# Window attention on one core: out products of a block's windows in one matmul, with the own window selected afterwards

## What is computed

```
qkv = jnp.einsum('nchw,oc->nohw', xw, qkv_w)
pooled = _avg_pool5(qkv)
msq = jnp.concatenate([qkv, pooled], axis=1)
msq = msq.reshape(N, -1, 3 * DIM, ws * ws).transpose(0, 1, 3, 2)
q = jax.nn.relu(msq[..., :DIM])
k = jax.nn.relu(msq[..., DIM:2 * DIM])
v = msq[..., 2 * DIM:]
v = jnp.pad(v, ((0, 0), (0, 0), (0, 0), (0, 1)), constant_values=1.0)
kv = jnp.einsum('ngld,nglm->ngdm', k, v)
out = jnp.einsum('ngld,ngdm->nglm', q, kv)
out = out[..., :-1] / (out[..., -1:] + 1e-15)
...
y = jnp.einsum('nchw,oc->nohw', out, proj_w)
inv = bn_gamma / jnp.sqrt(bn_var + BN_EPS)
y = y * inv[None, :, None, None] + (bn_beta - bn_mean * inv)[None, :, None, None]
```

## Time and profile before

| | |
|---|---|
| median of 3 runs | 887.09 us (884.8 to 888.21) |
| the profiled execution | 886.18 us |
| its span in the trace | 884.3 us |
| granted TensorE clock, mean | 0.998 |
| TensorE busy, matmuls | 848.4 us (96%) |
| VectorE busy | 699.9 us (79%) |
| GpSimd busy | 658.9 us (75%) |
| ScalarE busy | 480.9 us (54%) |
| TensorE matmul instructions | 28322 |

### The profile page before, as it was taken

One profiled execution on the slowest core, in us unless ns is written; L12 is line 12 of the kernel. 1 busy time (PEld: TensorE's weight loads), 2 busy tenths in 40 slices (PEclk: granted clock), 3 DMA queues, 4 the chain that ended last, 5 costly groups with the idle time before them and its releaser, 6 DMA issues.

```text
span 884.3 us, 63772 instructions
## 1 busy us (share of the span) xinstructions
PE 848.4 (96%) x28322; PEld 693.0 (78%) x28322; DVE 699.9 (79%) x1252; ACT 480.9 (54%) x1349; POOL 658.9 (75%) x1624
## 2 busy tenths in 40 slices
PE   0789999999999999999999999999999999999997
PEld 0568888888888888888888888888888888888885
DVE  7758888887778888888777888888777777777776
ACT  0346565646465655555555556565656564646563
POOL 2558787878787878777878777787878787878781
PEclk9999999999999999999999999999999999999999
DMA  6122322111123323111113232211111111111111
GB/s 236 40 77 81 103 84 82 49 47 48 47 69 97 91 94 98 51 48 47 49 50 99 86 98 88 82 51 48 48 50 46 49 48 47 48 47 48 47 49 47
DMA packets 39081, 60.06 MB, mean 68 GB/s; under 512 B 8560, under 2 KB 33648, under 8 KB 39024
## 3 DMA queue, kind: packets, MB, share of 16 engines
q1 hardware_dynamic: 39024, 59.52, 20.0%
HBM read 19.38 MB, written 18.87 MB: 43 GB/s over the span
## 4 chain that ended last, share of the span: by engine, by line
PE 94%; DVE 3%; issue 1%; DMA 1%; SPq 0%; ACT 0%; DVEq 0%
PE ps L703 24%; PE ps L687 17%; PE ps L659 14%; PE ps L668 9%; PE ps L675 9%; PE ps L787 7%; PE ps L778 6%; PE ps L789 4%; PE ps L676 4%; DVE stats L453 1%; DMA x_all<-x 0%; DVE kvc_full L561 0%; DVE kvc_pool L561 0%; DMA vm_full<-v_full 0%; DVE kvc_full L509 0%
## 5 line engine op out<-in xcount | busy, mean ns | idle before, releaser
L366 ACT ACTIVATE vm_pool<-ps,cst 128x256 f32<-128x256 f32 x576 | 230.1, 480 | 0.0
L376 ACT ACTIVATE q_full<-ps 128x384 f32<-128x384 f32 x96 | 47.2, 491 | 281.0 <-PE ps L675 281.0
L561 DVE TENSOR_TENSOR kvc_full<-ps,cst 128x864 f32<-128x864 f32 x192 | 193.2, 1048 | 4.7 <-PE ps L687 4.7
L561 DVE TENSOR_TENSOR kvc_pool<-ps,cst 128x864 f32<-128x864 f32 x192 | 193.2, 1048 | 0.5 <-PE ps L687 0.5
L286 POOL TENSOR_TENSOR xd<-x_all,mean_t 128x384 f32<-128x384 f32 x95 | 78.6, 827 | 154.3 <-PE ps L676 137.8
L659 PE MATMUL ps<-wkv_sb,xn 128*128 128x256 f32 x576 | 141.4, 382 | 23.1 <-DVE xn L517 23.1
L264 POOL TENSOR_TENSOR x_all<-y_pool,x_all 128x96 f32<-128x96 f32 x380 | 148.9, 424 | 12.7 <-DVE x_all L567 7.2
L659 PEld LDWEIGHTS ps<-wkv_sb,xn 128*128 128x128 f32 x576 | 109.4, 191 | 33.2 <-issue 23.0
L703 PEld LDWEIGHTS ps<-kvc_full,q_full 64*32 64x32 f32 x9216 | 108.3, 105 | 26.0 <-issue 26.0
L292 POOL TENSOR_TENSOR xn<-xd,rstd_t 128x96 f32<-128x96 f32 x380 | 121.8, 367 | 8.1 <-DVE xn L517 0.7
L703 PE MATMUL ps<-kvc_full,q_full 64*32 64x72 f32 x9216 | 125.0, 230 | 0.6 <-DVE kvc_pool L561 0.6
(11 more groups left out here) (74 smaller groups left out, 1316.2 us busy)
## 6 DMA issues: line engine op xcount, KB each, us to landing
vm_full<-v_full SPq DMA_DIRECT2D x384, 54.0 KB, 1.9
out<-x_all SPq DMA_DIRECT2D x96, 192.0 KB, 1.9
x_all<-x SPq DMA_DIRECT2D x36, 384.0 KB, 3.4
x_all<-x SPq DMA_DIRECT2D x6, 768.0 KB, 7.9
cst<-consts SPq DMA_DIRECT2D x1, 170.0 KB, 11.0
wkv_sb<-wkv SPq DMA_DIRECT2D x1, 128.0 KB, 10.8
o_sb<-proj SPq DMA_DIRECT2D x1, 128.0 KB, 10.1
wq_sb<-wq SPq DMA_DIRECT2D x1, 64.0 KB, 10.6
```

The costliest lines, as they stand in the source:

```text
L366: last = act.activation(heads[:, e, :, :, 0:D], src, ACT.Copy, scale=col(C_VP + e))
L561: last = dve.tensor_tensor(kvc[:, g], src.to_broadcast(shape), own, ALU.mult)
```

## The change

It changes how the out products of a quad's windows are told apart, who prepares their right-hand sides, and in which order and banks the steps run.

- An out product takes all windows of the quad at once: `out_tile` multiplies a quad's q (no zeros beside it) with the kv matrices of both windows, 144 columns in one matmul instead of two accumulated ones of 72. Each output row then holds a block for its own window and one for the other.
- The pooled ones (`pooled_out_tile`) contract over one quad's 32 partitions instead of 64, with the three windows' 108 columns, in two halves j = 0 and 1. So `kvc_pool` needs no copies with zeros for the other quad: `own_heads_pooled` is now four ScalarE instructions, one for each head column block, with a per-partition scale that is 1 for the channels of that head and 0 for others. It leaves VectorE.
- VectorE picks each row's own window: `select` copies window 0 and then, where a row belongs to window 1, copies window 1 over it (`copy_predicated`); `select_pooled` does so for three windows. Both write to `sel` in SBUF.
- One `divide` for full and pooled together reads `sel` and writes `o`.
- PSUM banks are free when the selection is over: `kv_products_pooled` waits for `sel_f`, `conv_kv` for `sel_p`. Banks: `TRF` and `Y_F` move to 7, `TRP` to 4, `Y_P` to 0.
- TensorE's order: pooled half 0, full, pooled half 1, then kv products. The transposes wait for `num`, `qm_f` and `qm_p`; the pooled projection waits for the first half of the next `kvc_full`; the full kv products wait for `copy_y_pooled`.
- VectorE's order: residual, select, select pooled, divide, `own_heads` of the next strip, statistics. ScalarE's: `own_heads_pooled` first, and `pooled_out` after `relu_k`.

The diff, cut to its core:

```diff
 def own_heads_pooled(s):
+    act.wait_ge(kv_p, s + 1)
+    wait(act, out_p, s)
+    src = ps[:, KVP:KVP + G, 0:HALF * KC].rearrange("p g (w c) -> p g w c", c=KC)
+    for h in range(4):
+        cols = slice(h * HC, (h + 1) * HC)
+        last = act.activation(kvc_pool[:, :, :, cols], src[:, :, :, cols], ACT.Copy,
+                              scale=col(C_HEAD + h))
+    last.then_inc(kvc_p, 1)
...
+def select(s):
+    dve.wait_ge(out_f, s + 1)
+    wait(dve, num, s)
+    dve.tensor_copy(sel_f_part, full_windows(0)).then_inc(win_f, 1)
+    dve.wait_ge(win_f, s + 1)
+    dve.copy_predicated(sel_f_part, rows_of(1, [P, G, TF, QG * KC]), full_windows(1)).then_inc(sel_f, 1)
+
+def select_pooled(s):
+    dve.wait_ge(out_p, s + 1)
+    dve.tensor_copy(sel_p_part, pooled_windows(0)).then_inc(win_p, 1)
+    dve.wait_ge(win_p, s + 1)
+    for e in range(1, WP):
+        dve.copy_predicated(sel_p_part, rows_of(WF + e, [P, G, TP * QG, KC]),
+                            pooled_windows(e)).then_inc(sel_p, 1)
+        dve.wait_ge(sel_p, (WP - 1) * s + e)
...
 def step(s, b, at, phase):
-    own_heads(s, False)
-    own_heads(s, True)
+    if not is_first(s):
+        residual(s - 1)
+    select(s)
+    select_pooled(s)
+    divide(s)
+    if not is_last(s):
+        own_heads(s + 1)
...
-    if not is_first(s):
-        residual(s - 1)
-    if not is_last(s):
-        divide(s, False)
-    divide(s, True)
...
+def out_tile(t):
+    n = WF * QG * KC
     for g in range(G):
         rows = slice(H64 * g, H64 * (g + 1))
         for c in range(4):
+            r, w = c // QG, (t * QG + c % QG) * WF
+            last = pe.matmul(ps[Q4 * c:Q4 * (c + 1), OUTF + g, t * n:(t + 1) * n],
+                             q_full[rows, 4 * t + c], kvc_full[rows, r, w:w + WF],
+                             start=True, stop=True)
...
+def pooled_out_tile(t, j):
+    n = WP * KC
+    for g in range(G):
+        rows, at = slice(H64 * g + Q4 * j, H64 * g + Q4 * (j + 1)), (t * QG + j) * n
...
 def kv_products_pooled(s):
     pe.wait_ge(vm_p, s + 1)
-    wait(pe, num_f, s)
+    wait(pe, sel_f, s)
...
 def transposes(s):
+    pe.wait_ge(num, s + 1)
     if not is_last(s):
-        pe.wait_ge(kvc_f, s + 2)
+        pe.wait_ge(qm_f, s + 2)
...
 def step(s, p):
...
     conv_kv_pooled(s + 1, p)
     if not is_first(s):
-        project(s - 1, out_next=True)
+        project(s - 1)
+    out_pooled(s, 0)
     out_products(s)
-    out_products_pooled(s)
+    out_pooled(s, 1)
     kv_products(s + 1)
     kv_products_pooled(s + 1)
     conv_q(s + 1, p)
```

More of the change, by code:

```diff
@@ L549, in link, with own_heads @@
                 dve.wait_ge(dv, s * DV + n)
[L551 to L556, removed]
+            def own_heads(s):
+                dve.wait_ge(kv_f, s + 1)
+                wait(dve, out_f, s)
                 shape = [P, HALF, QG, KC]
@@ L559, in own_heads @@
                 for g in range(G):
[L560 to L562 removed]
+                    src = ps[:, KVF + g, 0:HALF * KC].rearrange("p (w c) -> p w c", c=KC).unsqueeze(2)
+                    dve.tensor_tensor(kvc_full[:, g], src.to_broadcast(shape), own, ALU.mult).then_inc(kvc_f, 1)
             def residual(s):
@@ L584, in residual_pooled_last, with rows_of @@
                 last.then_inc(y_done, 1)
[L586 to L590, removed]
-                src = ps[:, bank:bank + G, 0:tiles * QG * KC].rearrange("p g (n c) -> p g n c", c=HC)
-                link(dve.tensor_scalar(den[:], src[:, :, :, D], DEN_EPS, None, ALU.add), s, step + 1)
-                link(dve.reciprocal(den[:], den[:]), s, step + 2)
-                wait(dve, turned, s)
-                heads = [P, G, tiles * QG * 4, D]
+            def rows_of(window, shape):
+                return col(C_WIN + window).bitcast(mybir.dt.uint32).unsqueeze(2).unsqueeze(3).to_broadcast(shape)
@@ L754, in out_products_pooled, with out_products, transposes @@
+            def out_products(s):
+                pe.wait_ge(kvc_f, G * (s + 1))
+                pe.nop(nofuse=True)
+                for t in range(TF):
+                    last = out_tile(t)
+                last.then_inc(out_f, 1)
+            def transposes(s):
+                pe.wait_ge(num, s + 1)
+                if not is_last(s):
+                    pe.wait_ge(qm_f, s + 2)
                 else:
                     pe.wait_ge(added_f, s)
-                    pe.wait_ge(y_copied, s)
@@ L758, in out_products_pooled @@
-                    pe.nop(nofuse=True)
-                for t in range(TP):
-                    for e in range(WP):
-                        last = out_tile(True, t, e)
-                last.then_inc(out_p, 1)
-            def transposes(s):
-                if not is_last(s):
-                    pe.wait_ge(kvc_f, s + 2)
-                else:
-                    pe.wait_ge(num_f, s + 1)
-                    pe.wait_ge(added_f, s)
-                    pe.wait_ge(y_copied, s)
-                for bank, o, n, pxs, columns, done in (
-                        (TRF, o_full, TF, P, C_IDENT, tr_f), (TRP, o_pool, TP, 4 * WP * PXP, C_PACK, tr_p)):
-                    if is_last(s) and o is o_pool:
-                        pe.wait_ge(num_p, s + 1)
-                    for t in range(n):
-                        last = pe.transpose(ps[:, bank, t * pxs:t * pxs + P], o[:, t].rearrange("p c g -> p (c g)"),
-                                            col(columns, P))
-                    last.then_inc(done, 1)
@@ L782, in project @@
-            def project(s, out_next=False):
+                for t in range(TF):
+                    last = pe.transpose(ps[:, TRF, t * P:(t + 1) * P], o[:, t].rearrange("p c g -> p (c g)"),
+                                        col(C_IDENT, P))
+                last.then_inc(tr_f, 1)
+                if not is_last(s):
+                    pe.wait_ge(qm_p, s + 2)
+                pxs = 4 * WP * PXP
+                for t in range(TP):
+                    last = pe.transpose(ps[:, TRP, t * pxs:t * pxs + P], o[:, TF + t].rearrange("p c g -> p (c g)"),
+                                        col(C_PACK, P))
```

136 lines of the change are left out of this document (74 added, 62 removed).

## The result

The changed kernel takes 938.42 us (median of 4 runs, 936.64 to 941.65) against 887.64 us of the kernel before beside it: a ratio of 1.058, 95% interval 1.0545 to 1.0621. It is slower by 5.8%. The forecast was 875 us with a range of 858 to 906, so the time lies outside it, and it moved the other way: slower instead of faster.

A forecast was written before the change was run, and what follows sets the result against it. TensorE was taken to bound the kernel, busy 96% of the span, 8.77 us a strip. From 886.2 us, 94 strips x 0.11 and 0.5 for start and tail were subtracted: 875 us, range 858 to 906.

The forecast's parts named there:

- the second loop, through the division: VectorE's copies, joint division and product up to TensorE's transposes: margin 0.08 us, 8.58 us as a loop of its own.
- the product of 640 elements at 0.83 us: VectorE's last division step, sized from 559 ns for 384 elements and 1.04 ns an element; ends at 5.49.
- GpSimd and the DMA queue keep their work: Work of GpSimd and the DMA queue taken as unchanged; spreading of values takes up to 2.4 us, in time.
- TensorE, what is removed: Out products per strip: 2.20 us replaced by 0.73 full and 0.74 pooled; TensorE's own work falls from 8.77 to 8.04 us.
- Changes of the shape: TensorE switching between whole-array, 32x32 and 64x32 tiles: three changes more a strip, 0.15 us each, bounds 0 and 0.18.
- Where VectorE's answer becomes late: TensorE's pooled kv products wait for VectorE's selection: a new wait of 0.17 us, next beat at 8.66 us.
- The predicated copies: VectorE's selection copies, taken at 1.04 ns an element: 0.60 us for 432 elements, 0.45 for 288.
- the bound taken from the residual: Dearer estimate for the predicated copy of 432 elements, from the residual's 0.62 us for 384: 0.67 us; 0.60 was taken.
- Rival 3: Predicated copies are dear and VectorE sets the beat: slower from 1.23 ns an element, 911 to 967 us; chance 0.26.
- Its sign for failure in the profile: In the trace after the change, TensorE's transposes wait for VectorE's product `o`; no size given.
- ScalarE: Four `kvc_pool` instructions of 0.46 us each, 1.5 us in all, hidden with 0.4 us to spare.
- Start and tail: First strip about -1.9 us, TensorE's early pauses 0 to -2, tail +2.5: together -0.5 us.

The follow-up runs named there:

- in one shape: Changed kernel with pooled out products contracted over 64 partitions instead of 32, so all small tiles are 64 rows by 32 columns (wrong pooled sum): 922.31 us.
- the kernel without the port's trouble: Changed kernel with the denominators and their reciprocals in PSUM, so the division's product reads only one operand from SBUF: 895.18 us, ratio to the kernel before 1.012.

## Why the prediction was wrong

The step that failed is one term of "the second loop, through the division": the product of 640 elements at 0.83 us. It was sized from the earlier trace rows, the old product of 384 from PSUM, and the rate is right, since 821 to 829 ns were measured wherever nothing stood in its way. What the term left out, at nothing and without a reason, is a wait: the change moves the numerators from PSUM to SBUF, which makes this instruction the first in the strip with two SBUF operands of some length, and GpSimd's subtraction starts at just that time. "GpSimd and the DMA queue keep their work" was true of the work and not of what it meets. The product took 1.33 us on average, 1.50 in most strips. With 1.33 the prediction's own loop through the division is 9.08 instead of 8.58, the beat 0.42 longer than the 8.66 forecast, and the sum 886.2 + 94 x 0.31 - 0.5 = 915 us: this step alone leaves the range.

- *TensorE, what is removed.* The 48 instructions of 144 columns keep the pace (0.77 in one shape, 0.73 foretold). The pooled halves take 0.40 in one shape, 0.37 foretold.
- *Changes of the shape.* Right: 0.15 was taken, 0.13 and 0.15 to 0.19 measured; the one in the loop is worth 13 us. Dropping this term would have given a false gain.
- *Where VectorE's answer becomes late.* The place was right, the size too small: 0.30 us of wait instead of 0.17. VectorE starts at 1.07 instead of 1.02, the predicated copy takes 0.66 instead of 0.60, and TensorE resumes 0.11 after it instead of 0.05: 2.48 instead of 2.30. This is the 0.17 us between the beat of 8.66 and the 8.83 of the kernel without the port's trouble, and 16 us of the time.
- *The predicated copies.* 659 ns for 432 elements, 486 for 288: 1.20 ns for each further element, instead of 1.04. The copy of 432 lies just under 0.67, the bound taken from the residual; I chose the wrong end. Alone it makes the beat 8.72 and the forecast 881 us, its slow end; no run separates it from the handoff.
- *The rivals.* Rival 3 named the right loop (VectorE sets the beat through the division, no cover beyond 0.08 us) and the wrong instruction. Its sign for failure in the profile, transposes that wait for the product `o`, is what the trace shows; its mechanism, copies at 1.23 ns or more, is not: at 1.20 that loop stays at 8.74 by the prediction's sum. A margin of 0.08 us between two loops should have carried more than 0.26, whatever the instruction.
- *ScalarE.* The four instructions of `kvc_pool` take 454 ns each (0.46 foretold) and are hidden.
- *Start and tail.* With the denominators in PSUM the second strip's full out products begin at 45.3 us (46.7 in the kernel before), and from the last strip's to the end it is 13.4 us (9.8 before): +2.2, where -0.5 was put down. Part of the tail is TensorE's clock. There it waits 4.14 us for the last division, the granted clock is 0.50 behind that (1.00 in the tail before), and the two instructions of the last full projection take 1.65 us instead of 0.81.

In sum: of the 63 us between forecast and time, 43 are the port, 16 the handoff with the dearer predicated copy (94 x 0.17), and the rest is mostly start and tail. The last two parts are read from single executions.

## What to carry to other kernels

When a change moves an operand of a VectorE instruction from PSUM to SBUF, look whether its other tensor operand lies there too, and what GpSimd reads at that moment: the instruction's own rate says nothing of it. Where the denominators can lie in unused PSUM columns, the meeting is avoided for little: here their sum takes 0.30 us instead of 0.23 and their reciprocal 0.67 instead of 0.65. And when two loops lie within a tenth of a microsecond, each edit that removes one wait shows the next: order, shapes, banks and DMA issues each took the place of the one before here.

## What the runs showed that I had not expected

- The contention goes both ways and is decided by who is first: 0.01 us late cost VectorE 0.67 us, 0.16 us early cost GpSimd 0.5 us. Against the denominators in PSUM the total is 43 us longer in one case and about 10 in the other.
- One small wait can close a loop over all engines: holding GpSimd's start for the division gave 1447 us, 54% more than the 938 of the changed kernel, without adding any work. Most of it is the loop, 14.2 us in the median strip; the mean of 14.8 holds the strips in which TensorE was granted the lower clock level for longer.
- A DMA issue took SyncE 0.46 to 0.60 us, and ScalarE 0.49 and 0.86 us; on an engine in the loop that is at least as dear as ScalarE's copy of 384 elements (0.49).
